# Layer 0 attention: adding finished output rows before the maxima, with copies and a rounding reordered in the first slots

## What is computed

```
x = x + tanh(g_xattn[0]) * L0_xattn(layernorm(x), ctx)      # 32 heads of 128
x = x + tanh(g_ffn[0])   * L0_ffn(layernorm(x))             # table-coded 4/8 bit weights
x = x + tanh(g_xattn[1]) * L1_xattn(layernorm(x), ctx)      # 32 query heads, 8 key heads
x = x + tanh(g_ffn[1])   * L1_ffn(layernorm(x))

L0_xattn:  xn = rmsnorm(x) * ln_weight
           q = xn @ w_q.T;  k = ctx @ w_k.T;  v = ctx @ w_v.T
           p = softmax(q k^T + position_bias, masked)
           out = x + (p v) @ w_out.T
```

## Time and profile before

| | us |
|---|---|
| median of 3 runs | 1715.7 (1715.33 to 1717.14) |
| profiled execution, its own time | 1714.45 |
| span of the profiled execution | 1712.6 |
| PE busy in the span | 1671.6 (98%) |
| DVE busy | 1193.6 (70%) |
| ACT busy | 1001.6 (58%) |
| POOL busy | 589.2 (34%) |
| granted TensorE clock, mean | 0.997 |

### The profile page before, as it was taken

How to read it: one execution, slowest core, us unless ns; L and a number is a source line. 1 busy time by engine, 2 the same in 40 slices (tenths; PEclk the granted TensorE clock), 3 DMA queues, 4 the chain that set the end, 5 groups by cost and what they waited for, 6 DMA issues and landing times.

```text
span 1712.6 us, 30969 instructions
## 1 busy us (share of the span) xinstructions
PE 1671.6 (98%) x10269; PEld 1483.0 (87%) x10269; DVE 1193.6 (70%) x2245; ACT 1001.6 (58%) x2540; POOL 589.2 (34%) x584
## 2 busy tenths in 40 slices
PE   8999999999889999999999999999999999999998
PEld 7999999999788888888887788888888888888886
DVE  6444446576687777877778876768676777777676
ACT  5344434345766767667676566665666656666563
POOL 2322223210324343343435433333333333333343
PEclk9999999999999999999999999999999999999999
DMA  6444433544323333333323010101011111111001
GB/s 221 174 147 165 153 147 147 190 161 156 101 73 107 111 110 101 119 99 113 107 85 128 23 61 16 58 25 61 22 51 34 49 37 46 37 37 40 13 7 50
DMA packets 80592, 153.31 MB, mean 90 GB/s; under 512 B 6545, under 2 KB 58129, under 8 KB 76945
## 3 DMA queue, kind: packets, MB, share of 16 engines
q1 hardware_dynamic: 80528, 152.50, 26.5%
HBM read 108.43 MB, written 44.04 MB: 89 GB/s over the span
## 4 chain that ended last, share of the span: by engine, by line
PE 83%; DVE 9%; ACT 4%; issue 2%; DMA 1%; POOL 1%; SPq 0%; DVEq 0%; ACTq 0%; POOLq 0%
PE bank L2046 21%; PE bank L1993 14%; PE bank L1995 14%; PE bank L1994 14%; PE bank L2222 6%; PE bank L2438 3%; PE bank L2257 2%; PE bank L2180 2%; PE bank L2339 2%; PE bank L2464 2%; PE bank L2168 1%; DVE qw_lo L1322 1%; DVE nmax L1543 1%; DVE sc L1541 1%; PE bank L2469 1%
## 5 line engine op out<-in xcount | busy, mean ns | idle before, releaser
L1993 PE MATMUL bank<-w_hi,xt_hi 128*128 (+2 forms) x512 | 178.0, 348 | 0.8 <-DVE qt_lo L1900 0.8
L748 POOL TENSOR_TENSOR p<-p,rn 128x512 f32<-128x512 f32 x128 | 133.1, 1041 | 122.7 <-DVE rn L1872 119.5
L691 POOL TENSOR_TENSOR pr<-pr,rn 128x512 f32<-128x512 f32 x64 | 66.6, 1041 | 313.5 <-DVE rn L1558 313.5
L1995 PE MATMUL bank<-w_hi,xt_lo 128*128 (+2 forms) x512 | 172.6, 337 | 0.0
L1994 PE MATMUL bank<-w_lo,xt_hi 128*128 (+2 forms) x512 | 171.3, 335 | 0.0
L1199 ACT ACTIVATE p<-bank,nb,q_r 128x256 f32<-128x256 f32 x256 | 141.0, 561 | 5.0 <-DVE nb L1867 2.6
L610 POOL TENSOR_TENSOR q_r<-q_ms,half 128x4 f32<-128x4 f32 x64 | 64.4, 1007 | 192.1 <-DVE q_ms L1846 192.1
L1047 ACT ACTIVATE pr<-sc,nmax 128x128 f32<-128x128 f32 x256 | 99.8, 391 | 48.9 <-DVE nmax L1543 48.5
L1993 PE MATMUL bank<-w0o_hi,ot_hi 128*128 128x512 f32 x256 | 106.0, 414 | 14.7 <-DVE residual L1550 12.5
L1993 PE MATMUL bank<-w_hi,ot_hi 128*128 (+1 forms) x256 | 106.1, 415 | 1.9 <-DVE ot_lo L1888 1.9
L610 POOL TENSOR_TENSOR k_r<-k_ms,half 128x2 f32<-128x2 f32 x64 | 56.8, 888 | 147.6 <-DVE k_ms L1825 147.6
(11 more groups left out here) (294 smaller groups left out, 5539.4 us busy)
## 6 DMA issues: line engine op xcount, KB each, us to landing
stage<-w SPq DMA_DIRECT2D x35, 512.0 KB, 3.3
keys_of_layer<-kout SPq DMA_DIRECT2D x16, 1024.0 KB, 4.5
values_of_layer<-vout SPq DMA_DIRECT2D x16, 1024.0 KB, 5.2
kt<-keys_of_layer SPq DMA_DIRECT2D x64, 256.0 KB, 3.2
vs<-values_of_layer SPq DMA_DIRECT2D x64, 256.0 KB, 2.8
vraw<-wv SPq DMA_DIRECT2D x10, 1024.0 KB, 6.7
kraw<-wk SPq DMA_DIRECT2D x16, 512.0 KB, 5.6
stage0o<-w SPq DMA_DIRECT2D x16, 512.0 KB, 4.2
```

What stands on the lines that cost most here:

```text
L691: pool.tensor_tensor(by4(pr), by4(pr), rn[:, :].unsqueeze(2).to_broadcast([P, 4, P]), ALU.mult).then_inc(norm_done, 1)
L748: pool.tensor_tensor(p1[:, half_p:half_p + 2, :], p1[:, half_p:half_p + 2, :], rn1[:, half_p:half_p + 2].unsqueeze(2).to_broadcast([P, 2, ...
L1993: nc.tensor.matmul(out_ap, l_hi, r_hi, start=(c == 0), stop=False)
L1995: op = nc.tensor.matmul(out_ap, l_lo, r_hi, start=False, stop=(c == n - 1))
```

## The change

Five edits, in the order of the program's stages.

1. POOL begins the sums of the first value weight at `t_lo_done >= 8` (the end of DVE's work on the context) in place of `kw_lo_done >= 4`. ACT rounds those sums before, no longer after, the copy L845 of the same group.
2. In slots 0 and 1 of the attention, the rounding of a query weight (ACT L1092) and its low part (DVE L1669) move from the end of slot 0 to slot 1, behind the exponentials. PE's two plain query projections of slot 1 are put on both sides of the transposes, and ACT's copies of them on both sides of the exponentials.
3. In slots 2 to 6, `accumulate` takes the rows of one projection later than before (i - 1 in place of i - 2) and stands near the end of the slot. Slot 7 has none.
4. From slot 8 to slot 59, `accumulate(i - 2)` stands before `maxima(i + 1)`.
5. PE's wait for `t_lo_done` 12 moves from ahead of the loop to the first product that needs it (p = 1). `row_stats(1, 0)` moves on DVE from slot 63 to behind `output_lo(U - 1)`.

```diff
@@ -650,7 +650,7 @@
                 if not last:
                     weight_sums(kraw, kraw_in, ksum_done, 2 * s + 2, 2 * s + 1)
 
-            pool.wait_ge(kw_lo_done, 4)
+            pool.wait_ge(t_lo_done, 8)
             weight_sums(vraw, vraw_in, vsum_done, 0, 0)
             weight_sums(kraw, kraw_in, ksum_done, 2, 1)
             weight_sums(vraw, vraw_in, vsum_done, 1, 1)
@@ -913,10 +913,10 @@
                     quarter12(s, 1)
                     part2(s, 2)
                 else:
-                    part2(s, 2)
                     act.wait_ge(vsum_done, 4)
                     act.wait_ge(product_done, 8)
                     nc.scalar.activation(vw_hi[:, S2:S4 + 1, :, :], vraw[:, S2:S4 + 1, :, :], ACT.Copy).then_inc(vw_hi_done, 1)
+                    part2(s, 2)
                 part4(s, 2)
                 part1(s, 3)
                 quarter12(s, 2)
@@ -1075,21 +1075,24 @@
                     return
                 if p == 0 and not first:
                     query_weight_late(n + 1)
+                if first and j == 1:
+                    queries_out(3)
                 if not (first and j == 0):
                     probabilities_copied(i)
                 if first and j == 0:
                     queries_out(2)
                 exponentials(i + 1)
-                if first and j > 0:
+                if first and j == 1:
+                    act.wait_ge(w_in[0], 32)
+                    nc.scalar.activation(w0_hi[0][1][:, :], stage0[0][:, :], ACT.Copy).then_inc(w_hi_done[0], 1)
+                    queries_out(4)
+                elif first and j > 1:
                     for k in QUERIES_IN_SLOT[j]:
                         queries_out(k + 1)
                 if not first:
                     query_part(n + 1, 1 - parity, p)
                 if not (first and j == 0):
                     output_hi(i, j - 1)
-                if first and j == 0:
-                    act.wait_ge(w_in[0], 32)
-                    nc.scalar.activation(w0_hi[0][1][:, :], stage0[0][:, :], ACT.Copy).then_inc(w_hi_done[0], 1)
                 if first and j == 3:
                     act.wait_ge(w_in[0], 48)
                     nc.scalar.activation(w0_hi[0][0][:, :], stage0[0][:, :], ACT.Copy).then_inc(w_hi_done[0], 1)
@@ -1622,6 +1625,13 @@
                 dve.wait_ge(diff_done, 7 if d == T1 else 5 + QUERY_DIFFERENCES.index(d))
                 low_part(qt_t_lo[:, d, :, :], raw_t(d), qt_t_hi[:, d, :, :], t_hi_done, 9 + QUERY_DIFFERENCES.index(d), t_lo_done)
 
+            ACCUMULATED_AHEAD = (2, 3, 4, 5, 6)
+
+            def accumulate_base(count, j):
+                if j < 3 + B // 2:
+                    dve.wait_ge(base_done, 2 * (j - 3) + 2)
+                accumulate(count, 2 * ((j - 3) % 4))
+
             def slot(t, j):
                 i, n, p, parity = BODY * t + j, 2 * t + j // 4, j % 4, (j // 4) % 2
                 first = isinstance(t, int) and t == 0
@@ -1640,20 +1650,15 @@
                     dequantise(n, p, i + 1)
                     inverse_sums(i + 1, 2 * p)
                     accumulate(i - 1, 2 * ((j - 2) % 4))
-                    if j == BODY - 1:
-                        dve.wait_ge(acc_done, U - 3)
-                        row_stats(1, 0)
                     return
                 if first and j == 0:
                     dve.wait_ge(kd_out, 16 * NG + 32 * EG)
                 if j == 0:
                     wait(dve, eq_done, 2 * BODY * t)
                     nc.vector.tensor_copy(code_pair[:, :], codes[:, bass.ds(2 * t, 2)]).then_inc(codes_ready, 1)
+                if not first:
+                    accumulate(i - 2, 2 * ((j - 3) % 4))
                 maxima(i + 1, j % 2)
-                if not (first and j < 3):
-                    if first and j < 3 + B // 2:
-                        dve.wait_ge(base_done, 2 * (j - 3) + 2)
-                    accumulate(i - 2, 2 * ((j - 3) % 4))
                 if first and j == 0:
                     residual_factors()
                     dve.wait_ge(valid_done, 1)
@@ -1662,18 +1667,22 @@
                 if active and p == 3:
                     quarter21_of_queries(n + 1, 1 - parity)
                 inverse_sums(i + 1, 2 * (j % 4))
-                if lag1:
-                    output_lo(i, (j - 1) % 2)
-                if first and j == 0:
+                if first and j == 1:
                     dve.wait_ge(w_hi_done[0], 2)
                     nc.vector.tensor_tensor(w0_lo[0][1][:, :], stage0[0][:, :], w0_hi[0][1][:, :].bitcast(fp32),
                                             ALU.subtract).then_inc(w_lo_done[0], 1)
+                if lag1:
+                    output_lo(i, (j - 1) % 2)
                 if first and j == 4:
                     dve.wait_ge(w_hi_done[0], 3)
                     nc.vector.tensor_tensor(w0_lo[0][0][:, :], stage0[0][:, :], w0_hi[0][0][:, :].bitcast(fp32),
                                             ALU.subtract).then_inc(w_lo_done[0], 1)
+                if first and j == 2:
+                    accumulate_base(i - 1, j + 1)
                 if first and j in (1, 2, 5, 6):
                     query_difference(QUERY_DIFFERENCES[(1, 2, 5, 6).index(j)])
+                if first and j in ACCUMULATED_AHEAD and j > 2:
+                    accumulate_base(i - 1, j + 1)
                 if first and j in LOW_IN_SLOT:
                     for d in LOW_IN_SLOT[j]:
                         query_difference_lo(d)
@@ -1728,6 +1737,8 @@
                 feed_forward(1, gate_lo[:, b:b + 1], b)
 
             output_lo(U - 1, (BODY - 2) % 2)
+            dve.wait_ge(acc_done, U - 3)
+            row_stats(1, 0)
             dve.wait_ge(acc_done, U - 2)
             row_stats(1, 1)
             dve.wait_ge(fbias_in, 16)
@@ -2233,6 +2244,7 @@
                     pe.wait_ge(c11_done, job)
                     query_product(2, 1, True)
                 if p == 1:
+                    pe.wait_ge(t_lo_done, 12)
                     pe.wait_ge(kw_lo_done, 2 * query_weight(n) + 2)
                     pe.wait_ge(part1_done, nth_part(job))
                     query_product(6, 0, False)
@@ -2283,11 +2295,12 @@
                     first_queries(1)
                 scores(t, j)
                 if first and j == 1:
-                    for k in QUERIES_IN_SLOT[1]:
-                        first_queries(k)
+                    first_queries(2)
                 if not (first and j == 0):
                     transposed_probabilities(i)
-                if first and j > 1:
+                if first and j == 1:
+                    first_queries(3)
+                elif first and j > 1:
                     for k in QUERIES_IN_SLOT[j]:
                         first_queries(k)
                 elif not first:
@@ -2311,7 +2324,6 @@
             for j in range(BODY):
                 slot(0, j)
             pe.wait_ge(qt_done, 4 * PLAIN)
-            pe.wait_ge(t_lo_done, 12)
             with pe.Fori(1, TL - 1) as t:
                 for j in range(BODY):
                     slot(t, j)
```

## The result

The changed kernel takes 1747.2 us (median of 3 runs), 1.0176 times the kernel before, 95% interval 1.0160 to 1.0191. The forecast was 1745 us. The profiled execution of the changed kernel took 1745.6 us, against 1714.45 before: +31.1.

A forecast was written before the change was run, and what follows sets the result against it. PE bounds the kernel before; with the pairs moved, DVE and ACT together do. 27.7 + 0.1 + 2.9 - 0.8 = +29.9 us on 1714.45 gives 1744.3, the median 1745.6, stated as 1745; all bounds 1733 to 1757, 8 in 10 within 1729 to 1756.

The forecast's parts named there:

- The pairs in slots 8 to 55: Accumulation pairs ahead of the maxima lengthen each four-slot group from 30.39 to 32.70 us, twelve groups: +27.7 us.
- the ring: Slots 8 to 55: DVE-ACT cycle from maxima to next maxima, 27.42 us per four slots, 32.70 with the moved pairs.
- What should show it: Profile signs: maxima of slots 8 and 56 about 392 us apart, `rn` waiting about 1.6 us, PE's share about 96%.
- PE's waits: Slots 8 to 56: the accumulation wait gone, waits of 1 to 2 us for POOL's scaled probabilities in its place.
- The spare time of the ring: Slots 8 to 55: without the pair, DVE and ACT have 2.97 us to spare per four slots against PE's 30.39.
- the break-even of 0.74 us a pair: Slots 8 to 55: moving the pairs breaks even only where each adds less than 2.97 / 4 = 0.74 us.
- PE's 5.6 us go: Slots 8 to 56: PE's twelve 0.46 us waits for DVE's accumulation, 5.6 us in all, disappear.
- the rival at 1700: Whole kernel: PE stays the bound, the pairs are hidden and PE's waits go, 15.5 us gained, 1700 us; chance 7%.
- Slots 56 to 59: Four slots without low parts take 30.2 us with the moved pairs, against 30.06: +0.1 us.
- Slots 0 to 7: Moved rounding -3.2, six pairs in series +7.9, cover -1.8: maxima of slot 8 later by +2.9 us, bounds -3 to +5.
- The start: First value sums: POOL starts earlier but takes turns with DVE on SBUF, -0.8 us; bounds -5.7 to +1.
- `row_stats`: Moved first-row statistics: PE's product up to 1.7 us earlier, same DVE work in sum; 0, between -1.7 and +0.7.

The follow-up runs named there:

- e1: The changed kernel with the accumulation pair of slots 8 to 59 put back behind the maxima, all else kept: 1716.3 us, ratio 1.0005 to the kernel before.
- e2: The kernel before with only the accumulation pair of slots 8 to 59 moved ahead of the maxima: 1745.4 us, ratio 1.0175.
- e9b: The changed kernel with the pair ahead of the maxima at p = 0, 1 and 2, not at p = 3: 1729.3 us, ratio 1.0080 to the kernel before.
- e4: The changed kernel with the pair ahead of the maxima at p = 1, 2 and 3, not at p = 0: 1742.1 us, ratio 1.0151 to the kernel before.
- e3: The changed kernel with the pair ahead of the maxima only at p = 2: 1714.7 us, ratio 0.9993 to the kernel before.
- e7: The kernel before with only the first rows' statistics moved behind the last accumulation but one: 1716.3 us, ratio 1.0005.
- e8: As e5, but POOL starts its first sums only when DVE has made its own four: 1714.3 us, ratio 0.9987 to the kernel before.
- e5: The kernel before with the start edit alone (POOL's earlier first value sums, ACT's earlier rounding): 1714.6 us, ratio 0.9986.
- e6: e1 with the accumulations of slots 3 to 7 and the first rows' statistics back as in the kernel before: 1711.1 us, ratio 0.9964 to the kernel before.
- e11b: e6 with POOL's first sums waiting for DVE's own four: 1711.0 us, ratio 0.9968 to the kernel before.

## Why the prediction was right

- **The pairs in slots 8 to 55**: +27.7 foreseen, +27.8 measured. The intervals between the maxima are 7.55, 8.71, 7.55 and 8.90 us, where the terms 6.23, 7.37, 6.23 and 7.59 with 1.32 each give 7.55, 8.69, 7.55 and 8.91. e1 and e2 show that the swap alone does it, e9b that the ring's sum holds where three pairs are moved.
- **What should show it**: `rn` waits 1.72 us where 1.6 was foreseen, PE's share is 96%, and slots 8 to 56 take 392.4 us where about 392 was.
- **PE's waits**: "PE's wait for the accumulation gone" was wrong. An engine that is late is waited for wherever its work stands: with DVE and ACT as the bound, PE comes early to the pair of p = 2 as to the probabilities. It does not enter the sum, since the ring sets the time. The 1 to 2 us foreseen for each group's probabilities were two waits of 0.6.
- **The spare time of the ring**: 2.97 us was too much. With the pair behind the maxima at p = 0 the ring is 0.88 longer (8.43 less 7.55 in e4; the 7.11 us from p = 0 on in e3 are 6.23 + 0.88), so the kernel before had 2.1 us to spare. The forecast said that the low part there fits under the exponentials; low part and pair together do not. The trace of the kernel before had the sign of it, in a slot with p = 0, on DVE and POOL:

```profile
661.25 1.41 DVE L1533 SCALAR_TENSOR_TENSOR wl<-eq,lut,wl 128x512 f32<-128x512 f32 x1 [0.19 <-ACT eq L1013]
```

```profile
660.94 1.16 POOL L669 TENSOR_TENSOR bm<-bias_sb,negm 128x512 f32<-128x512 f32 x1
```

  This term fell out of the sum, as all four pairs were moved, and so the break-even of 0.74 us a pair stands, for four pairs. For a change of three the same sum missed by 11 us (e4: 387.65 us, 376.6 by the uncorrected ring).
- **"PE's 5.6 us go"** (the gain of the rival at 1700): e3 takes that very wait away, and the group stays at 30.38 us. Even with room in the ring that gain was not there, but for 0.8 us in slots 56 to 59.
- **Slots 56 to 59**: +0.1 foreseen, +0.05 measured.
- **Slots 0 to 7**: +2.9 foreseen, +2.0 measured (79.91 us from slot 0 to slot 8 in place of 77.89). The six pairs were put at 6.1 us after cover and cost 4.5; the rounding was put at -3.2 and gave 2.5 against the kernel before (3.4 less 0.9), 1.4 against e7 and e8. The steps foreseen for slots 1 to 8 (-3.2, -2.1, -1.2, -1.2, 0, +0.3, +1.6, +2.9) were -3.4, -2.4, -1.5, -1.5, -0.3, -0.6, +0.8, +2.0: 0.3 better from slot 2 on, and from slot 5 to slot 6 another 0.6, where more was covered than read.
- **The start**: -0.8 foreseen. From the start of the context's last low part on DVE to PE's first transposes of the normed rows (near 400 us) the ten kernels with the new start take 373.2 to 376.3 us, 375.2 in the mean, and the three with the old one 376.2 to 377.1, 376.6 in the mean: about 1.3 less. e5's ratio gives 1.0 to 3.9. The stop of 4.0 us from 29.6 on (3.1 in e5) and DVE's stretched sums are as described. The Trainium skill ("SBUF — State Buffer", "Who interferes with whom") has a DVE instruction with two inputs in SBUF and a GpSimd one that reads SBUF exclude each other. This case's traces agree: DVE's sums take 1.4 us in e5 and 0.42 in e8, and `wl` at p = 0 takes 1.62 in e4 and 0.75 in e9b. The slow stretch behind the stop of the earlier trace rows, which only the start's lower bound uses, is longer than the 1.6 us of clock read from the earlier trace rows: half clock goes on to 46.6, 2.6 us of clock from 41.4 on.

```profile
44.60:46.60 2.00, 2.00 (x11) 2.00 (x11) 0.00 (x0) 0.41 (x1) 0.25 (x1) 0.50 0.41 168
```

- **`row_stats`**: 0 foreseen with +0.7 as its bound, and the bound is what the traces show: 0.6 to 0.8 us. The rest of the 3.2 us behind slot 60, some 2.5, goes with the two stretches of half clock, by the table of the thirteen traces. Whether the moved statistics bring such stretches about is not shown; e6 and e11b have two without them.
- **The range**: the upper end comes out as added (1757), the lower does not. With every lower bound at once (19 + 0.1 - 3 - 5.7 - 1.7) the sum is +8.7, 1724 us and not 1733.
- **The total**: the profiled +31.1 is +0.1 to slot 8, +27.8, +0.05 and 3.2 of which the forecast had none, while it had +2.1 to slot 8. That the total came out within 2.2 us of the foreseen 1745 owes something to these two cancelling, and that is luck.

## What to carry to other kernels

Before an instruction is moved ahead of a handover, follow the ring that the handover belongs to, through each engine, and compare its length with what the bound engine takes for the same loop: an instruction is free where it stands under another engine's work, and costs its whole length ahead of the handover once the spare time is used up. Do that sum with the new order for each slot of the loop, since three pairs cost 11.4 or 22.4 us here, depending on which one stayed. A small wait of the busiest engine is no gain waiting to be taken: look what comes next there when the waited-for step comes earlier.

## What the runs showed of the hardware that was not expected

- How much half clock an execution has differs between executions of one kernel: beside e5, on one chip, the kernel before ran 1719.65 us at a mean granted clock of 0.992 and 1714.12 us at 0.997. In the 13 profiled ones, of as many kernels, PE loses 5.1 to 10.2 us of full clock to it (windows of 1 us over the span, each counted by what PEclk lacks), in stretches at several of its stops. A stop of the same place and length is followed by one in one trace and not in another: PE waits 2.25 us near 976 us in the kernel before and goes on at full clock,

```profile
976.00:980.00 4.00, 3.38 (x18) 2.80 (x19) 3.93 (x9) 3.23 (x12) 1.88 (x3) 1.00 0.14 36
```

  and in e7, behind the same 2.25 us, it does not:

```profile
976.00:980.00 4.00, 3.72 (x14) 2.94 (x13) 3.97 (x10) 2.63 (x10) 1.16 (x2) 0.57 0.38 116
```

  A difference of 2 or 3 us between two of these profiled executions can be that alone. What decides it stays open.
- PE's stops of up to 1.1 us in slots 8 to 56 of the changed kernel, three in each group, brought no half clock at all.
- Two engines' use of SBUF at once can change a loop's time by where the two meet: `wl` lost 0.87 us in each group of e4 where POOL's `bm` started 0.1 us ahead of it, and nothing in e9b, where it started 1.0 us ahead and overlapped by 0.17.
